# Attention on one core: the cast, the subtraction and the store of a chunk's output stand four head steps later

## The chip, the cores and the metric

The kernel runs on one core of one Trainium2 chip. The metric is the device time of one launch, in microseconds. Its engines are named as the profile names them: PE is TensorE's matmuls and PEld its weight loads, DVE is VectorE, ACT is ScalarE, POOL is GpSimd, and SP is SyncE, which here only issues DMAs. Each engine works through its own instructions in order and waits on semaphores.

## The reference

One post-norm decoder layer over `x` of shape (2, 2048, 512), 16 heads of 32. Only the first third matters here, causal self-attention:

```python
qkv = x @ Wqkv.T
q, k, v = map(merge_heads, jnp.split(qkv, 3, axis=-1))
dots = jnp.einsum('bhid,bhjd->bhij', q, k) * dh ** (-0.5)
dots = jnp.where(causal_mask, -jnp.inf, dots)
attn = jax.nn.softmax(dots, axis=-1)
out = jnp.einsum('bhij,bhjd->bhid', attn, v)
x = _layernorm(x + out @ Wout.T + bout)
```

A cross-attention over 77 context rows and a layer of 8 experts with top-2 gates follow, each with a residual and a norm.

## The kernel before

The program has three stages, one after the other. `project` makes queries, keys and values and leaves them in DRAM. `self_attention` makes the attention output and leaves it in DRAM as `o_parts`, in two float16 halves that together hold more than one float16 can. `second_half` does all the rest. The change lies in `self_attention`.

The work is cut into 8 groups: 2 sequences by 4 sets of 4 heads. A group's 2048 query columns are 4 chunks of 512 columns. Because the mask is causal, chunk `c` needs only the key tiles 0 to 4c+3 of 128 rows, so the chunks have 4, 8, 12 and 16 tiles, 40 in all. Each tile is done for 4 heads, which gives 160 head steps for a group. `KU` lists the tiles, `VU` the head steps. The chunks' last head steps are 15, 47, 95 and 159.

All engines walk through the same head steps `s`, each in its own function `step`. An item with lag L of head step p stands at `s = p + L`. The order is written out by hand with such lags:

- TensorE, lag 0 (`scores`, L865): keys times queries of one head and tile into one of three banks `st_ps`. It waits until the exponential three steps before has read its bank. Diagonal tiles get a mask by a second matmul (L868).
- ScalarE, lag 0 (L762): the exponential of that bank into `probs`. The buffer `probs` holds 5 tiles, and an exponential waits for the addition and the values product of the tile five before.
- GpSimd (L637): every fourth step it adds a tile of exponentials of all four heads onto `total`. Of the tiles off the diagonal each third is left to TensorE (L899), and a chunk's first tile is no addition of its own; the second tile's addition reads both.
- TensorE, `values` (L885) at lag 4 into `o_ps`, and `totals` (L909) at lag 12, which sums `total` over the rows for the softmax's denominators. `totals` waits for the last addition of the chunk.
- Besides, TensorE makes scores the other way round for later chunks (`aux`, L851) and VectorE takes row maxima of them (L804, L808), about one for each head step. A chunk's maxima are turned, cut in two by ScalarE and VectorE (L745, L797), and SP moves them into `q_pair` (`turn`, L678). They must be there before the chunk's first scores.

The end of a chunk is a chain over several engines, in lags after the chunk's last head step:

- `TAKEN` 5 and 13: ScalarE copies `o_ps` to `o_raw` (L768) and the denominators to `den` (L772).
- `DEN_MOVED` 14: SP moves the denominators to `inv_small` (L698). `INVERTED` 22: VectorE takes the reciprocals (L822). `INV_STORED` 24 and `INV_LOADED` 30: SP stores them to DRAM and loads them spread over the rows as `inv` (L702, L707).
- `SCALED` 38: GpSimd multiplies `o_raw` by `inv` into `o_sb` (L647), after the subtraction of the chunk before.
- `UPPER` 46: ScalarE casts `o_sb` to float16, the upper half of `o_out` (L777). It waits for the multiply.
- `LOWER` 49: GpSimd subtracts that upper half from `o_sb` into the lower half of `o_out` (L652). It waits for the cast.
- `STORED` 51: SP stores `o_out` to `o_parts` (L714). It waits for the subtraction.

`TAIL` is `STORED + 1`. The first `TAIL` steps run as a prologue, in which the maxima are spread evenly, and then come four laps of two groups each, all written out. SP also loads the next groups' keys and queries, one chunk at a time, at the absolute lags `REFILLED`: for a group's frame these stand at steps 54, 86, 93 and 100, the last with the values of the group (L666, L670). In the last lap at `s == TAIL` SP waits for the earlier laps' stores and issues `load_rows` (L941, L942), 2 MB for the next stage. `if REFILLED[c] <= TAIL: load(1, 1, c)` ahead of the laps covers a reload whose step falls into the prologue.

Of the kernel before, what the change touches and what calls it, by code (L numbers as in the profile page):

```python
# [401 lines left out]
def self_attention(nc, S, x_rows, q_parts, k_parts, v_rows, o_parts, inv_rows):  # L402
# [37 lines left out]
    INV_STORED = INVERTED + 2  # L440
    INV_LOADED = INV_STORED + 6
    SCALED = INV_LOADED + 8
    UPPER = SCALED + 8
    LOWER = UPPER + 3
    STORED = LOWER + 2
    TAIL = STORED + 1
# [81 lines left out]
    def chunk_at(s, lag, first, end):  # L528

        k = tile_at(s, lag, first, end)  # L530
        return k // NKU * CPB + CHUNK_OF[k % NKU] if k is not None and k % NKU in CHUNK_OF else None
# [11 lines left out]
    with ExitStack() as stack:  # L543
# [188 lines left out]
        def _(act):  # L732
# [15 lines left out]
            def step(i, s, first, end):  # L748
# [21 lines left out]
                if c is not None:  # L770
                    act.wait_ge(den_ready.sem, den_ready.at(i, c))
                    nc.scalar.activation(den[:, c % 2], den_ps[:], ACT.Copy, scale=1.0 / XS).then_inc(den_taken.sem, 1)  # L772
                c = chunk_at(s, UPPER, first, end)
                if c is not None:
# [744 lines left out]
def layer(nc, x_rows, xT, ctxT, mask, wqkvT, woutT, bout, wq, bq, wk, bk, wv, bv, wo, bo, w1, b1, w2, b2, centroids,  # L1519
          routeT, out):  # L1520

    dram = lambda name, shape, dt: nc.dram_tensor(name, shape, dt).ap()
    q_parts, k_parts, o_parts = (dram(n, [2, D, N], F16) for n in ("q_parts", "k_parts", "o_parts"))
    v_rows = dram("v_rows", [N, D], F32)
    inv_rows = dram("inv_rows", [2, HG, CH], F32)
    w_parts = dram("w_parts", [2 * KT, P, 2, KT * D], F16)
    k_blocks, v_ctx = dram("k_blocks", [B, P, NG * HG * S2], F32), dram("v_ctx", [B, S2, D], F32)
    with ExitStack() as stack:
        S = lasting(nc, stack)
        smalls = [(S["bout_bc"][:], bout.partition_broadcast(P)), (S["bo_bc"][:], bo.partition_broadcast(P)),  # L1530
                  (S["bq_sb"][:], bq), (S["b1_sb"][:], b1), (S["b2_sb"][:], b2)]
        project(nc, S, xT, wqkvT, ctxT, wk, wv, woutT, wq, wo, w1, w2, centroids, routeT, smalls, bk, bv,
                q_parts, k_parts, v_rows, w_parts, k_blocks, v_ctx)
        self_attention(nc, S, x_rows, q_parts, k_parts, v_rows, o_parts, inv_rows)
        second_half(nc, S, x_rows, o_parts, mask, w_parts, k_blocks, v_ctx, out)
# [68 lines left out]
```

## Time and profile before

| | |
|---|---|
| median of 3 runs | 2617.73 us (2617.07 to 2618.23) |
| the profiled execution's own time | 2619.38 us |
| its span | 2617.6 us |
| TensorE matmuls busy | 2421.4 us, 93% |
| VectorE busy | 1718.9 us, 66% |
| GpSimd busy | 1118.5 us, 43%, nearly all of it in the attention |
| ScalarE busy | 1102.5 us, 42% |
| attention | from about 285 to 1353 us of the span |

Busy shares are averages over the whole span, and the stages differ much, so the attention has to be read by itself. A line of a timeline begins with the start in microseconds from the start of the span and the duration. `x2` means two instructions merged into one line, and the brackets at the end give the idle time of the engine before it and what released it. Matmuls overlap in their ends, so a full PE row is not a full engine. The granted clock is a share of full speed: 1.00 is 2.4 GHz, 0.50 is 1.2 GHz.

### The profile page before, as it was taken

To read this page: it belongs to the slowest core of one execution; us is meant where nothing else is said; L and a number is where in the kernel's file an instruction comes from. 1 tells how busy PE (TensorE), PEld (TensorE's weight loads), DVE (VectorE), ACT (ScalarE), POOL (GpSimd) and SP (SyncE) were. 2 spreads that over 40 slices of the span, in tenths; PEclk is the share of its full clock that TensorE was granted. 3 is DMA by queue.
4 is the path that set the end of the run, shared out by engine and by line. 5 is a ranking of instruction groups with operands and counts; after the bars stand their busy time and mean duration, and the time that the engine had idled before them with its cause. 6 is when DMAs were issued, how large, how long until landed. Compare 5 with 4: busy or idle time off the path is not lost. (4 is left out here: it accounts for less than half of the span.)

```text
span 2617.6 us, 36273 instructions
## 1 busy us (share of the span) xinstructions
PE 2421.4 (93%) x13556; PEld 1013.8 (39%) x13556; DVE 1718.9 (66%) x3957; ACT 1102.5 (42%) x2066; POOL 1118.5 (43%) x404
## 2 busy tenths in 40 slices
PE   7999799999999999989946799999999999999998
PEld 3444223333323232323214354454445444454543
DVE  5433687777767677767405577767677776767665
ACT  4331156666666666666623242332324232322320
POOL 0000379989898989898952111102111211101100
PEclk9999799999999999999977899999999999999999
DMA  7864312212121213040021101010100101010000
GB/s 254 298 206 156 92 38 54 58 42 58 42 63 37 71 33 86 14 118 16 24 104 50 45 1 62 1 46 17 40 22 1 62 1 46 17 46 17 1 17 17
DMA packets 130443, 155.00 MB, mean 59 GB/s; under 512 B 19838, under 2 KB 98174, under 8 KB 129245
## 3 DMA queue, kind: packets, MB, share of 16 engines
q1 hardware_dynamic: 130269, 152.69, 19.1%
q8 instruction: 108, 1.77, 0.3%
q14 instruction: 66, 0.54, 0.1%
HBM read 99.96 MB, written 52.17 MB: 58 GB/s over the span
## 5 line engine op out<-in xcount | busy, mean ns | idle before, releaser
L762 ACT ACTIVATE probs<-st_ps 128x512 f32<-128x512 f32 (+3 forms) x1280 | 610.2, 535 | 339.9 <-PE st_ps L865 194.4
L637 POOL TENSOR_TENSOR total<-total,probs 128x2048 f32<-128x2048 f32 (+3 forms) x200 | 706.2, 3531 | 77.2 <-ACT probs L762 58.6
L804 DVE TENSOR_REDUCE seg_max<-s_ps 128x1 f32<-128x512 f32 x768 | 505.9, 685 | 139.2 <-PE s_ps L851 137.0
L865 PE MATMUL st_ps<-q_pair,k_pair 98*128 98x512 f16 (+3 forms) x1280 | 445.2, 362 | 34.9 <-ACT probs L762 28.8
L851 PE MATMUL s_ps<-k_pair,q_pair 96*128 96x512 f16 (+3 forms) x1280 | 446.1, 364 | 33.1 <-DVE seg_max L804 11.6
L1429 PE MATMUL fps<-x2T,w_p_hi 128*128 128x512 f16 x1024 | 317.3, 379 | 0.0
L885 PE MATMUL o_ps<-probs,v_sb 128*32 128x512 f32 (+3 forms) x2560 | 307.2, 553 | 0.0
L808 DVE CUSTOM_DVE_ANT_0 s_ps<-s_ps,later 128x384 f32<-128x384 f32 (+3 forms) x512 | 250.7, 497 | 85.8 <-issue 82.4
L1429 PE MATMUL fps<-w_p_hi,hT 128*128 128x512 f16 x1024 | 305.9, 380 | 0.0
L865 PEld LDWEIGHTS st_ps<-q_pair,k_pair 98*128 98x128 f16 x1280 | 125.0, 99 | 345.3 <-ACT probs L762 244.8
L1133 POOL TENSOR_TENSOR rstd<-rstd,keep_power 128x4 f32<-128x4 f32 x24 | 26.0, 1085 | 542.0 <-DVE rstd L1254 542.0
L1216 ACT ACTIVATE hidden<-fps,keep_b_sb 128x512 f32<-128x512 f32 x128 | 86.4, 686 | 377.0 <-PE fps L1429 374.8
L1148 POOL TENSOR_TENSOR soft<-soft,ssum 128x1232 f32<-128x1232 f32 x32 | 72.9, 2287 | 392.6 <-DVE ssum L1284 392.6
L851 PEld LDWEIGHTS s_ps<-k_pair,q_pair 96*128 96x128 f16 x1280 | 126.6, 100 | 235.6 <-DVE seg_max L804 119.5
L1391 DVE SCALAR_TENSOR_TENSOR x<-fps,gates_un,x 128x512 f32<-128x512 f32 x256 | 183.5, 742 | 34.4 <-PE fps L1429 31.5
L1429 PE MATMUL fps<-w_p_lo,hT 128*128 128x512 f16 x512 | 194.7, 380 | 0.0
L1429 PE MATMUL fps<-x2T,w_p_lo 128*128 128x512 f16 x512 | 194.0, 379 | 0.0
L1380 DVE TENSOR_SCALAR hT<-hidden 128x512 f16<-128x512 f32 x128 | 92.1, 719 | 105.7 <-ACT hidden L1216 105.0
L637 POOL TENSOR_TENSOR total<-probs 128x2048 f32<-128x2048 f32 (+1 forms) x32 | 136.4, 4263 | 46.4 <-ACT probs L762 46.4
L1429 PEld LDWEIGHTS fps<-x2T,w_p_hi 128*128 128x128 f16 x1024 | 100.1, 98 | 128.9 <-issue 5.9
L1429 PEld LDWEIGHTS fps<-w_p_hi,hT 128*128 128x128 f16 x1024 | 98.1, 98 | 131.0 <-issue 20.9
L1187 ACT ACTIVATE soft<-soft 128x1232 f32<-128x1232 f32 x32 | 39.4, 1231 | 201.0 <-DVE soft L1277 201.0
(164 smaller groups left out, 3403.5 us busy)
## 6 DMA issues: line engine op xcount, KB each, us to landing
k_pair<-k_parts SPq DMA_DIRECT2D x96, 128.0 KB, 3.9
q_pair<-q_parts SPq DMA_DIRECT2D x96, 128.0 KB, 4.9
x_raw<-xT_in SPq DMA_DIRECT2D x8, 1024.0 KB, 6.1
q_parts<-qk_out SPq DMA_DIRECT2D x32, 256.0 KB, 3.7
k_parts<-qk_out SPq DMA_DIRECT2D x32, 256.0 KB, 3.8
piece_raw<-w_in SPq DMA_DIRECT2D x8, 1024.0 KB, 8.7
v_rows<-v_out SPq DMA_DIRECT2D x32, 256.0 KB, 2.1
w_parts<-piece_cut SPq DMA_DIRECT2D x8, 1024.0 KB, 5.6
```

Source lines behind the costliest of these rows:

```text
L637: last = nc.gpsimd.tensor_tensor(summed[:, :, off:], other[:, :, off:], probs[:, k % NP, :, off:], ALU.add)
L762: nc.scalar.activation(probs[:, k % NP, h, off:], st_ps[:, p % (2 * NVU) % RING, off:], ACT.Exp, scale=SCALE).then_inc(exp_done.sem, 1)
L804: nc.vector.reduce_max(highest, s_ps[:, slot], AX.X).then_inc(s_read.sem, 1)
L808: nc.vector.tensor_tensor_reduce(s_ps[:, slot, 0:width], s_ps[:, slot, 0:width], later[:, CH - width:CH], 1.0, MASKED, ALU.add, ALU.max, h ...
L851: nc.tensor.matmul(s_ps[:, slot, 0:width], q_pair[a][0:NR, c, h, j * P:(j + 1) * P], k_pair[a][0:NR, h, s * CH:s * CH + width], start=True ...
L865: last = nc.tensor.matmul(st_ps[:, slot, off:], k_pair[a][:, h, kt * P:(kt + 1) * P], q_pair[a][:, c, h, off:], start=True, stop=not diagonal)
L885: last = nc.tensor.matmul(o_ps[out, off:], v_sb[a][:, kt, out], probs[:, k % NP, h, off:], start=(kt == 0), stop=final)
L1148: nc.gpsimd.tensor_tensor(soft[:, j], soft[:, j], ssum[:, j, :].rearrange("p (h a) -> p h a", a=1).broadcast_to([P, H, S2]), ALU.mult).the ...
L1216: nc.scalar.activation(hidden[:, n % 2], fps[:, (u * NUNIT + f) % FB], ACT.Gelu, bias=W["b1_sb"][:, n:n + 1], scale=UN).then_inc(gelu_done ...
L1380: nc.vector.tensor_scalar(hT[:, 0, e % 2, j], hidden[:, n % 2], XS, None, ALU.mult).then_inc(h_hi.sem, 1)
L1391: nc.vector.scalar_tensor_tensor(x2[q][:, j], bank, gates_un[q][:, j, e:e + 1], x2[q][:, j], ALU.mult, ALU.add).then_inc(added.sem, 1)
L1429: last = nc.tensor.matmul(bank, lhs(a, t), rhs(b, t), start=(n == 0), stop=(n == len(steps) - 1))
```

## The change

ScalarE's cast of a chunk's output stands at lag 50 instead of 46. `LOWER`, `STORED` and `TAIL` are set from it, so the subtraction moves from 49 to 53, the store from 51 to 55, and `TAIL` from 52 to 56. `SCALED` and everything ahead of it in the chain stay, and so do the reloads' lags. `REFILLED[0]` is 55, so `REFILLED[0] <= TAIL` now holds, and the reload of chunk 0 for the second group is issued ahead of the laps. Of items that share a step SP takes the reloads before the store.

```diff
     INV_STORED = INVERTED + 2
     INV_LOADED = INV_STORED + 6
     SCALED = INV_LOADED + 8
-    UPPER = SCALED + 8
+    UPPER = SCALED + 12
     LOWER = UPPER + 3
     STORED = LOWER + 2
     TAIL = STORED + 1
```

## Rows read from the trace of the kernel before

**Rows 1.** One window: us, busy us of PE, PEld, DVE, ACT, POOL, granted clock, DMA

```profile
400.00:1200.00 800.00, 763.38 (x4986) 243.81 (x4988) 587.97 (x1902) 511.88 (x1103) 724.20 (x239) 0.96 0.22 55
```

**Rows 2.** List of waits, 300 to 1400 us: total us, times, longest us

```profile
ACT o_out L777 <- POOL o_sb L647: 45.1, 17, 9.8
...
PE st_ps L865 <- ACT probs L762: 28.8, 17, 4.4
...
POOL total L637 <- ACT probs L762: 105.0, 49, 16.3
```

**Rows 3.** Timeline of ScalarE: start us, duration, operation, idle time before

```profile
515.91 0.45 ACT L762 ACTIVATE probs<-st_ps 128x128 f32<-128x128 f32 x2 [0.68 <-PE st_ps L868]
520.70 0.63 ACT L777 ACTIVATE o_out<-o_sb 128x512 f16<-128x512 f32 x1 [4.34 <-POOL o_sb L647]
...
523.68 0.60 ACT L762 ACTIVATE probs<-st_ps 128x512 f32<-128x512 f32 x1
```

**Rows 4.** Timeline of GpSimd, second group

```profile
519.41 1.26 POOL L647 TENSOR_TENSOR o_sb<-o_raw,inv 128x512 f32<-128x512 f32 x1
520.63 7.33 POOL L637 TENSOR_TENSOR total<-total,probs 128x1536 f32<-128x1536 f32 x3
...
529.02 4.52 POOL L637 TENSOR_TENSOR total<-probs 128x2048 f32<-128x2048 f32 x1
...
537.64 9.22 POOL L637 TENSOR_TENSOR total<-total,probs 128x2048 f32<-128x2048 f32 x2 [4.09 <-ACT probs L762]
...
590.75 4.53 POOL L637 TENSOR_TENSOR total<-probs 128x2048 f32<-128x2048 f32 x1 [2.05 <-ACT probs L762]
597.30 4.54 POOL L637 TENSOR_TENSOR total<-total,probs 128x2048 f32<-128x2048 f32 x1 [2.02 <-ACT probs L762]
```

**Rows 5.** Timeline of TensorE's matmuls, first, second and last group

```profile
396.29 0.39 PE L865 MATMUL st_ps<-q_pair,k_pair 98*128 98x512 f16 x1 [2.50 <-ACT probs L762]
...
521.55 0.61 PE L865 MATMUL st_ps<-q_pair,k_pair 98*128 98x512 f16 x1 [3.80 <-ACT probs L762]
...
528.33 1.94 PE L885 MATMUL o_ps<-probs,v_sb 128*32 128x512 f32 x8
...
533.61 1.04 PE L909 MATMUL den_ps<-total,ones 128*32 128x512 f32 x8
...
1338.20 1.94 PE L909 MATMUL den_ps<-total,ones 128*32 128x512 f32 x8 [11.54 <-POOL total L637]
```

**Rows 6.** Windows of 2 us in the second group (columns as in rows 1)

```profile
522.00:524.00 2.00, 2.00 (x10) 0.64 (x12) 1.24 (x6) 1.66 (x4) 2.00 (x1) 0.50 0.00 0
...
530.00:532.00 2.00, 1.78 (x9) 0.53 (x5) 0.73 (x3) 1.00 (x2) 2.00 (x1) 0.70 0.77 239
```

**Rows 7.** Timeline of VectorE: a masked maximum, 512 wide

```profile
525.88 0.69 DVE L808 CUSTOM_DVE_ANT_0 s_ps<-s_ps,later 128x512 f32<-128x512 f32 x1 [0.23 <-issue]
526.50 0.14 DVE L808 DVE_READ_ACCUMULATOR2_ANT seg_max<- 128x1 f32 x1
```

**Rows 8.** Two idle times of TensorE and the 3 us behind each

```profile
1179.35 0.34 PE L851 MATMUL s_ps<-k_pair,q_pair 96*128 96x384 f16 x1 [2.28 <-DVE seg_max L804]
...
1615.63 0.60 PE L1498 MATMUL cps<-keep_ident,gates 128*8 128x128 f32 x4 [1.60 <-DVE gates L1366]
...
1179.35:1182.35 3.00, 2.79 (x10) 0.83 (x14) 2.88 (x11) 1.19 (x2) 0.00 (x0) 0.57 0.10 29
1615.63:1618.63 3.00, 3.00 (x16) 1.52 (x17) 2.88 (x8) 1.87 (x2) 0.00 (x0) 1.00 0.02 5
```

**Rows 9.** SP's issue of the maxima's rows; their landing times (64 DMAs)

```profile
514.32 1.21 SPq L678 DMA_DIRECT2D q_pair<-max_rows  x2
...
DMA to landing us min/median/max: 1.7/1.9/9.1
```

**Rows 10.** Seventh group: SP's issue of load_rows and VectorE's wait

```profile
1124.84 0.39 SPq L941 DMA_DIRECT2D keep_x<-x_rows_in  x1
...
1137.11 0.25 DVE L822 RECIPROCAL inv_small<-inv_small 128x16 f32<-128x16 f32 x1 [4.86 <-DMA inv_small<-den]
```

## The prediction

> **What bounds the kernel now.** I read the window of the attention first. Over 800 us in its middle the matmul row is busy 763 us, GpSimd 724, VectorE 588 and ScalarE 512 [rows 1]. TensorE and GpSimd are both nearly full, so the question is which wait makes one stand while the other has work. The list of waits for 300 to 1400 us answers it: ScalarE stood 45.1 us in front of the very cast that is moved, 17 times, waiting for GpSimd's multiply `o_sb`; the matmuls stood 28.8 us behind ScalarE's exponentials, the largest wait of a matmul in the attention proper; and GpSimd itself waited 105.0 us for exponentials [rows 2]. So GpSimd is late at some places and idle at others.
>
> The timeline of one group (a group is 160 head steps, 126.7 us; this is the second of eight) shows the loop. A chunk's last step is 15, 47, 95 or 159 of its group. With `UPPER` = 46 the cast of chunk 1 stands at step 93, GpSimd's multiply for it (`SCALED` = 38) at step 85. ScalarE ended the exponential of step 93 at 516.36 us and then stood 4.34 us for the multiply, which began at 519.41 and ended at 520.67 [rows 3, 4]. TensorE may be only three score banks ahead (`RING` = 3), so it ran dry: 3.80 us idle [rows 5]. After it the granted clock was 0.50 of full (1.2 GHz, not 2.4) until about 531 us [rows 6]; eight values matmuls took 1.94 us there [rows 5]. Groups 2 to 5 repeat this; the first has a smaller wait, 2.50 us [rows 5], and a shorter slow stretch.
>
> Chunks 0 and 2 find their multiply done. For chunk 3 of the group before, ScalarE hardly stands. The longest of the 17 waits, 9.8 us [rows 2], is at the end, after all scores, where nothing is left to delay but the chain itself.
>
> **The change, part by part.** `UPPER` goes from 46 to 50, `LOWER` 49 to 53, `STORED` 51 to 55, `TAIL` 52 to 56. No instruction is added or removed in the steady part: 32 casts, 32 subtractions, 32 stores as before.
>
> *ScalarE.* The cast of chunk 1 stands at step 97, behind four more exponentials: 94 and 95, 128 wide, whose scores were there (0.56 us together), and 96 and 97, 512 wide at 0.60 us [rows 3], the first a microsecond after 516.4 because its scores come behind a values step. ScalarE is at the cast at about 518.7 instead of 516.4, and the multiply still ends at 520.67: a wait of 2.0 us is left of 4.34. TensorE meanwhile can issue scores up to step 100 instead of 96. In this stretch VectorE paces it too: one 512-wide masked maximum takes 0.69 + 0.14 us [rows 7]. I put TensorE's idle time at 1.7 us. Then, does the clock fall? Idle 2.28 us was followed by 0.57 of full clock, idle 1.60 us by 1.00 [rows 8], the same seven times over in the second half. 1.7 is by far nearer to the second, so I take: it stays high.
>
> By the Trainium skill (TensorE: Matmul & The Clock Gate, "What's actually happening") throttled is the default state and activity releases it, which speaks against counting on a rest of idle time being free. The rows agree that long idle times end at the lower level; they also show that short ones don't. If the page's warning held for this rest, rival B below would be the result.
>
> *What limits the gain.* GpSimd. From 597.30 us it runs without a gap through chunk 1's multiply to the last addition of chunk 2; in the group shown this chain ends 520.63 + 7.33 = 527.96 us. TensorE needs that sum at step 107 (`TOTALS`) and was there at 533.61 [rows 4, 5]. It can come 5.65 us earlier and no more. Does it? After the cast (521.3 us) ScalarE owes the exponentials 98 to 104 and one copy at 0.55 to 0.60 us; scores 104 come at about 524.6 instead of 530.2 (528.33 + 1.94), the totals at about 527.4. That is just under GpSimd's 527.96. So GpSimd decides, TensorE stands some 0.5 us more, and the gain is 5.65 us. Of it 3.8 us is the stall and 1.85 us the slow clock.
>
> Is it given back? GpSimd waits for exponentials three times later in the group: 4.09, 2.05 and 2.02 us [rows 4], beside two short waits. It loses these waits as ScalarE comes earlier, so it is 4.0 us earlier at 537.64 and 5.6 by 597.30, where it meets ScalarE again, with 2.5 us or more of idle time left. Exponentials wait for additions five tiles back; for tile 29 that addition ends at 529.02 + 4.52 = 533.54, and its exponential would come at about 535.6. Both sides hold. The gain repeats in each group.
>
> *GpSimd's queue.* The subtraction (1.16 us) moves four steps. For chunks 1 and 3 the step passed (100, 52) begins a chunk and has no addition, so its place is the same. For chunks 0 and 2 it comes after one addition of 4.5 us. All sums needed later come the same or 1.2 us earlier. Chunk 3's subtraction stands directly before chunk 0's multiply, which waits for it; its cast comes about 3 us before it is wanted. Nothing.
>
> *SP's queue.* SP runs ahead of the others and stands only on its waits, so an order change moves DMAs a lot. Chunk 3's store (step 54) now stands behind the reload of chunk 0 (also 54), and chunk 1's store (102) behind the reload of chunk 3 and the values (100). These reloads go out about 11 us earlier, and the rows behind the values' 1 MB no longer wait. Chunk 0's store (70) is released 4.5 us later, and behind it stand chunk 1's `inv_rows` store and load, used 15 us later, and the reload of chunk 1: 768 KB that now leave just ahead of the maxima's rows at 514.32 us. Those rows took 1.9 us to land in the median and 9.1 at worst [rows 9]. A lateness of up to 2 us vanishes in ScalarE's remaining wait. I take nothing for it.
>
> *Seventh group.* There `load_rows` (2 MB) stood at step 52 in front of the 768 KB reload, both in front of chunk 1's denominators; VectorE stood 4.86 us for them and TensorE 3.95, and a further 2.28 later [rows 8, 10]. Now the reload leaves before. 768 KB less in front is about 3.4 us (2.8 MB took 12.3 us from 1124.84 to 1137.1). With GpSimd's gaps there (2.5 and 3.8 us) I take 7 us for the group, between 4 and 8.
>
> *First and last group.* First: 2.5 us. The first 56 steps now carry 101 maxima tiles instead of 96 over 52; VectorE paces them either way, and the second chunk's rows come a step later: a loss of 0 to 1 us, I take 0.5. One 768 KB reload moves to the start, when the other loads are done. Last: TensorE ends waiting 11.54 us for GpSimd's total [rows 5], which has had no gap since the 2.0 us one early in that group. ScalarE's wait in it is worth 0: GpSimd is the bound to the end.
>
> *Sum.* 2.5 + 5 x 5.3 (5.65 less 0.35 for the handover from GpSimd) + 7 + 0 - 0.5 = 35.5; I round it down to 34.5 for places where the three engines nearly tie. The profiled execution took 2619.4 us for a span of 2617.6: 2584.9 by its own time, 2583.2 from the median of the runs, 2617.7. I say 2585.
>
> **Rivals.**
> A, the above: 2577 to 2592. Chance 0.57.
>
> B, *the clock still falls* at the remaining wait. For it: the level fell after 2.28 us and my 1.7 is an estimate. Then the 1.85 us of slow clock stay in six groups, and the time past step 107 loses perhaps as much again in half of them: 34.5 less 11 to 17, so 2595 to 2602. Chance 0.18.
>
> C, *the wait only moves*: exponentials run faster than I think between 516 and 519, or earlier gains eat the four steps, so that about 3 us of ScalarE wait stay. The gain is 1.5 to 2.5 us in a group: 2600 to 2608. Against it: four exponentials take at least 0.56 + 2 x 0.60 = 1.76 us [rows 3]. Chance 0.11.
>
> D, *GpSimd is the bound throughout*, and its work is the same: within 2 us of 2617.7. Against it: 8.2 us of waits in the group shown [rows 4]. For it: some of them may be forced by the order. Chance 0.06. The Trainium skill (Perfetto Trace Analysis, "Identifying the Most-Contended Engine") takes occupancy as a fair measure for GpSimd and not for matmuls, and would name GpSimd here; it would give this rival's time if taken for every stretch. The trace has GpSimd at 91% and waiting, so it agrees in part only.
>
> E, *slower*: the maxima's rows of chunk 3 land late because the reload of chunk 1 now goes just before them. At 9.1 us, 7.2 over the median, 2.0 are absorbed; 5.2 us of idle time and 1.85 of slow clock stand against 5.65 saved, so 1.4 us lost in each of seven groups: 2628. It decides from about 7.7 us to landing. Chance 0.04. The remaining 0.04 is for gains by ways that I don't see.
>
> **Numbers.** Range 2576 to 2603: A, B and the nearer part of C, 0.8. Differences under 0.2% (5 us) can't be told from no change. Faster 0.90 (A, B, C and the rest), same 0.06 (D), slower 0.04 (E).
>
> **What the changed kernel's profile would show.** ScalarE's wait before the cast falls from 45.1 to 20 to 28 us, 9.8 of them at the end; TensorE's wait for exponentials from 28.8 to under 15; the slices' clock near 1.0 through the attention; GpSimd's waits for exponentials from 105 to about 65; a new wait of 0 to 1 us before the totals of chunk 2; the step from one group's totals to the next 121 us instead of 126.7. I am wrong if the clock still drops once a group, if TensorE waits long for `max_rows`, or if GpSimd's gaps stay as they are.

## The result, and the profile after

| | before | changed |
|---|---|---|
| median of 4 runs each | 2617.98 us (2617.07 to 2622.35) | 2584.26 us (2582.06 to 2586.10) |
| span of the profiled execution | 2617.6 us | 2582.4 us |
| ratio | | 0.987, 95% interval 0.9856 to 0.9885 |

The forecast was 2585, the range 2576 to 2603. The changed kernel is faster, by 33.7 us in the medians.

The list of waits of the changed kernel for 300 to 1400 us (us in total, times, longest) answers to [rows 2]:

```profile
ACT o_out L777 <- POOL o_sb L647: 23.0, 9, 9.9
PE st_ps L865 <- ACT probs L762: 16.5, 16, 3.0
PE den_ps L909 <- POOL total L637: 13.3, 6, 10.9
ACT probs L762 <- POOL total L637: 6.3, 4, 3.0
PE st_ps L865 <- issue: 5.0, 1, 5.0
POOL total L637 <- ACT probs L762: 68.0, 25, 18.2
```

ScalarE stood 23.0 us before the cast instead of 45.1, TensorE 16.5 behind exponentials instead of 28.8, GpSimd 68.0 instead of 105.0. The third line is new in its length: TensorE now stands for GpSimd's sum at the totals, 10.9 us of it at the very end.

The timeline of the changed kernel shows the same place of the second group as [rows 3, 5], then two of GpSimd's waits that answer to [rows 4]:

```profile
518.88 0.63 ACT L777 ACTIVATE o_out<-o_sb 128x512 f16<-128x512 f32 x1 [1.55 <-POOL o_sb L647]
...
520.05 0.39 PE L865 MATMUL st_ps<-q_pair,k_pair 98*128 98x512 f16 x1 [1.34 <-ACT probs L762]
...
526.21 1.07 PE L909 MATMUL den_ps<-total,ones 128*32 128x512 f32 x8 [0.49 <-POOL total L637]
...
583.38 4.53 POOL L637 TENSOR_TENSOR total<-probs 128x2048 f32<-128x2048 f32 x1 [1.49 <-ACT probs L762]
589.94 9.21 POOL L637 TENSOR_TENSOR total<-total,probs 128x2048 f32<-128x2048 f32 x2 [2.03 <-ACT probs L762]
```

And its windows there, with the columns of [rows 1], then the long window that answers to [rows 1]:

```profile
520.00:522.00 2.00, 1.95 (x10) 0.50 (x14) 1.30 (x7) 2.00 (x5) 2.00 (x1) 1.00 0.56 144
522.00:524.00 2.00, 1.71 (x14) 0.42 (x7) 1.73 (x9) 1.94 (x4) 1.86 (x2) 1.00 0.87 178
...
400.00:1200.00 800.00, 777.43 (x5239) 251.33 (x5242) 610.09 (x1975) 535.06 (x1158) 755.14 (x251) 1.00 0.22 55
```

In this group the cast waits 1.55 us, TensorE 1.34 instead of 3.80, and the clock stays at full (2.4 GHz) where it was at half. The totals come 7.40 us earlier in the trace (533.61 less 526.21), and GpSimd's busy time in the 800 us rises from 724 to 755.

The clock did not stay up in every group. The mean of 800 us rounds to 1.00 and hides two short falls to half, in groups 3 and 6, behind idle times of TensorE of 1.52 and 1.69 us. The first of them in the timeline, then windows of the two groups:

```profile
641.49 0.39 PE L865 MATMUL st_ps<-q_pair,k_pair 98*128 98x512 f16 x1 [1.52 <-ACT probs L762]
...
642.00:644.00 2.00, 2.00 (x13) 0.40 (x12) 1.86 (x8) 2.00 (x5) 1.86 (x2) 0.71 0.89 174
644.00:646.00 2.00, 2.00 (x12) 0.49 (x5) 0.37 (x3) 0.76 (x2) 2.00 (x1) 0.50 0.87 132
...
1008.00:1010.00 2.00, 2.00 (x10) 0.31 (x10) 1.37 (x6) 1.36 (x3) 1.86 (x2) 0.52 0.69 122
```

In groups 2, 4, 5 and 7, behind 1.34, 1.58, 1.19 and 1.63 us, it stayed at full.

To see where the time came from, I take the starts of the matmuls of L909 and subtract them from the same ones of the kernel before. One number for each group, at the totals of its chunk 2 (10 steps after the place that the cast of chunk 1 has now) and of chunk 3:

| us earlier than before | group 1 | 2 | 3 | 4 | 5 | 6 | 7 | 8 |
|---|---|---|---|---|---|---|---|---|
| changed, chunk 2 | 0.79 | 7.40 | 11.93 | 17.03 | 22.02 | 26.34 | 30.40 | 35.59 |
| changed, chunk 3 | 1.88 | 7.37 | 11.93 | 17.01 | 21.99 | 26.34 | 34.43 | 34.39 |

So the groups gave 1.9, 5.5, 4.6, 5.1, 5.0, 4.4, 8.1 and nothing; of groups 2 to 6 the two that gave least, 3 and 6, are those in which the clock fell. Apart from the first, the seventh and the last group, the lead grows only between the totals of a group's chunk 3 and those of the next one's chunk 2, the stretch in which the cast stands, and is kept for the rest. The first totals of all are 2.68 us later than before, so the first group made some 4.5 us and lost 2.7.

### The profile page after: what moved, and what is told of

Same layout as the page of the kernel before. It is cut to its first block and busy times, and to the rows that moved or that the text cites. A ratio compares the mean times of both kernels' runs of the same rounds, so it can differ in the third digit from the quotient of the medians.

```text
span 2582.4 us, 36273 instructions
## 1 busy us (share of the span) xinstructions
PE 2400.6 (93%) x13556; PEld 1007.0 (39%) x13556; DVE 1714.1 (66%) x3957; ACT 1102.6 (43%) x2066; POOL 1118.8 (43%) x404
## 5 line engine op out<-in xcount | busy, mean ns | idle before, releaser
L851 PE MATMUL s_ps<-k_pair,q_pair 96*128 96x512 f16 (+3 forms) x1280 | 435.0, 355 | 25.9 <-DMA q_pair<-q_parts 11.4
L865 PE MATMUL st_ps<-q_pair,k_pair 98*128 98x512 f16 (+3 forms) x1280 | 434.4, 353 | 25.7 <-ACT probs L762 16.5
```

The costliest lines, as they stand in the source:

```text
L851: nc.tensor.matmul(s_ps[:, slot, 0:width], q_pair[a][0:NR, c, h, j * P:(j + 1) * P], k_pair[a][0:NR, h, s * CH:s * CH + width], start=True ...
L865: last = nc.tensor.matmul(st_ps[:, slot, off:], k_pair[a][:, h, kt * P:(kt + 1) * P], q_pair[a][:, c, h, off:], start=True, stop=not diagonal)
```

## The experiments

The theory with which I went in: the cast's place makes the whole gain, because it takes away TensorE's idle time and the slow clock, and GpSimd's chain sets its size. The rivals: that the subtraction, the store and `TAIL` do part of it, and that the remaining wait, not GpSimd, sets the size. The theory fell with the first run.

**The cast alone**

```diff
-    UPPER = SCALED + 8
-    LOWER = UPPER + 3
-    STORED = LOWER + 2
+    UPPER = SCALED + 12
+    LOWER = SCALED + 11
+    STORED = SCALED + 13
```

> ScalarE's cast alone stands four steps later; GpSimd's subtraction, the store and TAIL stay. Theory 1 (the cast's place in ScalarE's queue is the cause): groups 0 to 5 gain as in the changed kernel, some 27 us, the start loses nothing, and the seventh group keeps VectorE's 4.9 us wait for the denominators and gains 0 to 2 us. About 2590 us; ScalarE's wait before the cast 20 to 25 us. Theory 2 (SP's order, with reloads 11 us earlier, is the cause): no change in the middle groups, 2616 to 2620 us.

Measured: 2616.39 us against 2620.28 for the kernel before beside it, ratio 0.9985 (0.9976 to 0.9995). Most of the gain isn't there: 2590 was expected by the first theory. The time is the one that the second theory gave, but not its picture of middle groups without a change. ScalarE's wait before the cast is down to 21.5 us. From its list of waits:

```profile
DVE inv_small L822 <- DMA inv_small<-den: 94.6, 10, 47.5
PE s_ps L851 <- DVE seg_max L804: 26.0, 36, 3.8
POOL total L637 <- ACT probs L762: 99.7, 53, 15.8
```

In the changed kernel the first of these is 66.4 us, 3 times. The numbers at L909 say where it goes: at chunk 2 this kernel is ahead by 2.84, 6.23, 6.46, 5.83 and 5.38 us in groups 2 to 6, but at the chunk 3 right behind only by 0.93, 1.36, 0.79, 1.05 and 2.23. It makes 4 to 6 us in each group and gives 2 to 6 back before the next totals. The timeline of SP, VectorE and TensorE of this kernel in the fourth group, where most is given back:

```profile
781.44 0.38 SPq L714 DMA_DIRECT2D o_parts<-o_out  x1
781.86 1.44 SPq L666 DMA_DIRECT2D k_pair<-k_parts  x3
783.34 1.38 SPq L666 DMA_DIRECT2D q_pair<-q_parts  x3
784.76 0.43 SPq L670 DMA_DIRECT2D v_sb<-v_rows  x1
785.24 5.92 SPq L678 DMA_DIRECT2D q_pair<-max_rows  x2
791.20 0.59 SPq L698 DMA_DIRECT2D inv_small<-den  x1
...
795.34 0.25 DVE L822 RECIPROCAL inv_small<-inv_small 128x16 f32<-128x16 f32 x1 [4.63 <-DMA inv_small<-den]
...
796.20 0.34 PE L851 MATMUL s_ps<-k_pair,q_pair 96*128 96x384 f16 x1 [3.80 <-DVE seg_max L804]
```

And its window behind the last line, with the columns of [rows 1]:

```profile
798.00:800.00 2.00, 2.00 (x11) 0.24 (x9) 1.55 (x5) 1.01 (x2) 0.77 (x1) 0.50 0.24 88
```

SP takes its items in order. Its store of chunk 1 waits for GpSimd's subtraction, which ends at 781.4. Behind it stand the reload of chunk 3, the values, two moves of maxima and the denominators of chunk 2. The two moves of maxima take 5.92 us to issue instead of the 1.16 of the changed kernel, and their maxima were ready at 779.7 us, so this is no wait for them; what differs is that the reload and the values' 1 MB were issued just in front. So the denominators leave at 791.20 and VectorE stands 4.63 us for them. Until then it frees no bank of the scores made the other way round, and TensorE stands 3.80 us for VectorE. The stall that the cast's place took away is back 22 us after its old place, at a granted clock of 0.50. In groups 1 to 6 VectorE's wait is 1.82 to 4.63 us.

The kernel before has the same order in SP's queue. Its fourth group:

```profile
786.86 5.53 SPq L678 DMA_DIRECT2D q_pair<-max_rows  x2
792.43 0.59 SPq L698 DMA_DIRECT2D inv_small<-den  x1
...
797.01 0.25 DVE L822 RECIPROCAL inv_small<-inv_small 128x16 f32<-128x16 f32 x1
```

The denominators left 1.23 us later there, but VectorE came to the reciprocals only at 797.01 us and did not wait for them. In the first and the seventh group it did wait, 1.42 and 3.11 us:

```profile
417.31 0.25 DVE L822 RECIPROCAL inv_small<-inv_small 128x16 f32<-128x16 f32 x1 [1.42 <-DMA inv_small<-den]
1178.50 0.25 DVE L822 RECIPROCAL inv_small<-inv_small 128x16 f32<-128x16 f32 x1 [3.11 <-DMA inv_small<-den]
```

These are the groups with the short stall at the cast (2.50 us) and with none of a microsecond or more.

**The subtraction, the store and `TAIL` without the cast** (`UPPER = SCALED + 8`, `LOWER = SCALED + 15`, `STORED = SCALED + 17`)

> The cast stays at its place; the subtraction, the store and TAIL stand four steps later. Theory 1: the 3.8 us idle time and the slow clock stay once a group, ScalarE's wait stays near 45 us; only the seventh group gains, 6 to 8 us, and the start loses 1 to 2. About 2612 us. Theory 2 (SP's order is the cause): near 2584 us.

Measured: 2615.22 us, ratio 0.9984 (0.9974 to 0.9993). ScalarE's wait before the cast is 48.3 us, TensorE's for exponentials 27.3. Through groups 2 to 6 it stays within 1 us of the kernel before; in the profile its 4 us come in the seventh group, where 6 to 8 were expected. So one part alone gives 4 us, the other alone 5, and both together 34.

**Cast and reload, all else as before.** The edit of the cast alone, and the reload of chunk 3 with the values four steps earlier, which puts it ahead of chunk 1's store:

```diff
-    REFILLED = [DEN_MOVED + n for n in (41, 73, 80, 87)]
+    REFILLED = [DEN_MOVED + n for n in (41, 73, 80, 83)]
```

> The kernel before with the cast alone four steps later and the reload of chunk 3 with the values at head step 96 in place of 100, so ahead of chunk 1's store (step 98) in SP's queue. Cast alone gained 5 to 5.7 us at every group's totals of chunk 2 and lost it again within 12 steps, where VectorE waits for the denominators that stand in the queue behind 1.8 MB of reload. Theory A (that queue is the whole of the loss): the gain stays in all groups, the second stall of the seventh group goes too; the first, at step 69, stays: 2586 to 2594 us. Rival B (something else in the later store or subtraction is needed): near cast alone, 2610 to 2617.

Measured: 2584.89 us, ratio 0.987 (0.9855 to 0.9885), the whole gain, a microsecond more than the expectation. SP in its fourth group:

```profile
771.37 0.38 SPq L714 DMA_DIRECT2D o_parts<-o_out  x1
771.79 1.16 SPq L678 DMA_DIRECT2D q_pair<-max_rows  x2
772.99 0.59 SPq L698 DMA_DIRECT2D inv_small<-den  x1
```

Now the moves take 1.16 us, and the denominators leave 1.6 us behind the store instead of 9.8.

**Cast and values only.** The cast alone, and the values loaded with chunk 2 instead of chunk 3 (`if c == CPB - 2:`); the keys and queries of chunk 3 stay behind the store.

> Cast alone four steps later, and the 1 MB of values loaded with the reload of chunk 2 (step 93) in place of chunk 3's (100), so ahead of the store; the 768 KB of chunk 3 stay behind it. If the values' 2048 short pieces hold the queue (the maxima's rows take 5.6 us to issue behind them), most of the gain stays: 2588 to 2600 us. If 768 KB are enough to make the denominators late: 2605 to 2617.

Measured: 2585.12 us, ratio 0.9868 (0.9853 to 0.9883). SP in the fourth group:

```profile
772.08 1.38 SPq L666 DMA_DIRECT2D q_pair<-q_parts  x3
773.50 1.15 SPq L678 DMA_DIRECT2D q_pair<-max_rows  x2
774.69 0.59 SPq L698 DMA_DIRECT2D inv_small<-den  x1
```

The moves take 1.15 us although 768 KB still stand just in front of them. So the 768 KB alone don't hold them up, and the values' 1 MB has to be there too. Whether the values would do it alone no run shows.

**The changed kernel with that reload behind the store again**

```diff
-    REFILLED = [DEN_MOVED + n for n in (41, 73, 80, 87)]
+    REFILLED = [DEN_MOVED + n for n in (41, 73, 80, 91)]
```

> The changed kernel with only the reload of chunk 3 and the values put back behind chunk 1's store (step 104 in place of 100). Theory A: VectorE waits 2 to 4.5 us for the denominators once a group again, and about 5 us a group are given back: 2606 to 2616 us, the seventh group's first stall stays away. Rival B: 2584.

Measured: 2613.17 us, ratio 0.9977 (0.9968 to 0.9986). 6 us of the gain are left. SP and TensorE in the timeline of its fourth group:

```profile
784.37 0.43 SPq L670 DMA_DIRECT2D v_sb<-v_rows  x1
784.85 5.81 SPq L678 DMA_DIRECT2D q_pair<-max_rows  x2
790.70 0.59 SPq L698 DMA_DIRECT2D inv_small<-den  x1
...
795.67 0.34 PE L851 MATMUL s_ps<-k_pair,q_pair 96*128 96x384 f16 x1 [3.66 <-DVE seg_max L804]
```

And from its list of waits:

```profile
DVE inv_small L822 <- DMA inv_small<-den: 90.5, 10, 47.6
```

The same stall at the same place. The four runs agree from both sides: the gain is there when the values leave ahead of chunk 1's store, and gone when they leave behind it.

**Cast and store moved, the subtraction not** (`UPPER = SCALED + 12`, `LOWER = SCALED + 11`, `STORED = SCALED + 17`)

> Cast and store (with TAIL) four steps later, the subtraction at its old place. Both theories of SP's order: as the changed kernel, 2583 to 2586 us. Rival (the subtraction's place matters for GpSimd's queue): 5 us or more slower than that.

Measured: 2587.03 us, ratio 0.9877 (0.9861 to 0.9894). That is 2.8 us above the changed kernel and 1 above what was expected, with intervals of the ratios that overlap. In the profiles the last totals are 1.65 us behind those of the changed kernel. The clock fell in other groups here (2, 4 and 7), so the profile doesn't settle whether the subtraction's place has a part in it.

**The cast two steps later still** (`UPPER = SCALED + 14`, `LOWER` and `STORED` as in the changed kernel)

> The cast at lag 52 in place of 50; subtraction, store and TAIL as in the changed kernel. Theory 1 (GpSimd's sum of chunk 2 decides, the 1.3 to 1.7 us that TensorE still idles at the cast are not lost twice): the wait at the cast falls to below 0.7 us a group and TensorE waits 1.5 to 2 us more at the totals instead; time within 3 us of the changed kernel, 2581 to 2587. Rival (the remaining wait at the cast costs what it shows): 1.3 us less in each of seven groups, about 2575. Rival (the idle time, now in one piece before the totals, drops the clock): 2590 to 2596.

Measured: 2582.93 us, ratio 0.9859 (0.9842 to 0.9875), no different from the changed kernel. ScalarE's wait before the cast goes from 23.0 to 12.9 us and TensorE's for exponentials from 16.5 to 7.5, but TensorE's wait for GpSimd at the totals grows from 13.3 to 18.6. The wait that is left at the cast costs nothing that these times show; GpSimd's chain is the bound.

**All of it by two steps instead of four** (`UPPER = SCALED + 10`, the rest behind it as before)

> The cast at lag 48, half the way (subtraction 51, store 53, TAIL 54). ScalarE gains only the two 128-wide exponentials, 0.5 us, so it waits about 3.8 us; TensorE can issue two more steps, about 1 us, and idles about 2.8 us. Theory 1 with the clock as a term: the clock still falls once a group, each middle group gains about 1 us and the seventh its 6 to 8: 2603 to 2608 us. Rival (the gain goes with the steps): half of it, about 2600, with the clock up in most groups.

Measured: 2600.3 us, ratio 0.9926 (0.9911 to 0.994), 20 us or some six tenths of the gain. My theory said 2603 to 2608, the rival 2600 with the clock up in most groups; the time is the rival's, and the clock fell in every one of groups 2 to 6. The stall of the second group in its timeline, and the window behind it:

```profile
518.98 0.39 PE L865 MATMUL st_ps<-q_pair,k_pair 98*128 98x512 f16 x1 [3.34 <-ACT probs L762]
...
520.34 0.63 PE L865 MATMUL st_ps<-q_pair,k_pair 98*128 98x512 f16 x1
```

```profile
520.00:522.00 2.00, 2.00 (x9) 0.73 (x6) 1.37 (x7) 1.37 (x4) 1.86 (x2) 0.50 0.72 135
522.00:524.00 2.00, 2.00 (x13) 0.57 (x11) 1.83 (x10) 1.79 (x4) 1.86 (x2) 0.77 0.88 191
```

TensorE is idle for 3.34 us, and a microsecond after it starts again the granted clock is 0.50. Two steps shorten this stall by 0.5 us and the slow stretch behind it by more: it is over before 524 us here, and was 0.70 between 530 and 532 us in the kernel before [rows 6]. The theory had only counted whether the clock falls, not for how long.

**GpSimd relieved of one tile.** The changed kernel, with tile 7 of chunk 2 left to TensorE's L899:

```diff
-    POOLED = [[n for n, (k, kt) in enumerate(KU) if k == c and (kt >= c * TT or kt % 3 != 2)]
+    POOLED = [[n for n, (k, kt) in enumerate(KU) if k == c and (kt >= c * TT or (kt % 3 != 2 and (c, kt) != (2, 7)))]
```

> The changed kernel, with one tile of chunk 2 (the eighth) summed by TensorE in place of GpSimd: 4.5 us less for GpSimd, 0.9 us more for TensorE in each group. Theory (GpSimd's chain decides when TensorE may pass the totals of chunk 2): the waits at the cast of chunk 1 go away, the period of a group falls by 1 us, and the last group, bound by GpSimd to the end, by 3 to 5 us: 2572 to 2578. Rival (TensorE is the bound by now): 0.9 us more in each group, about 2590.

Measured: 2573.93 us, ratio 0.9829 (0.9814 to 0.9843), 10 us better than the changed kernel. ScalarE waits before the cast only at the end (9.7 us, once), TensorE 3.4 us for exponentials, and a group takes about 120 us. GpSimd's waits are back at 100.6. GpSimd has 4.5 us of work less in a group, TensorE a little more, and TensorE is now the bound. So GpSimd was the bound of the changed kernel where the clock stayed up. A part of the 10 us is the clock, which doesn't fall in groups 2 to 7 of this kernel.

In its first group it loses ground at one place, a late move of maxima and a slow clock behind it, here in the timeline and in a window:

```profile
397.59 0.39 PE L865 MATMUL st_ps<-q_pair,k_pair 98*128 98x512 f16 x1 [1.59 <-DMA q_pair<-max_rows]
...
402.00:404.00 2.00, 2.00 (x9) 0.57 (x11) 1.70 (x10) 1.61 (x3) 0.30 (x1) 0.50 0.78 191
```

The changed kernel has no such wait there and a full clock. Against it this kernel is 0.7 us ahead at the totals of chunk 1 and 4.1 behind at those of chunk 2.

**The reload of chunk 0 in its step instead of ahead of the laps**

```diff
+                    if first is not None and s == REFILLED[c] - 1:
+                        load(1, 1, c)
```

and without the lines ahead of the laps.

> The changed kernel, with the first reload of chunk 0 back at head step 54 of the first group in place of ahead of the laps. Theory: this reload, issued right behind the first rows of maxima, made them land late; TensorE's idle time before the first scores falls from 5.0 to 3.4 us and all later comes 1.6 us earlier: about 2582.6 us. Rival (the loss at the start is from the other spread of the maxima, or from outside the attention): no difference, 2584, and 5.0 us stays.

Measured: 2582.44 us, ratio 0.986 (0.9843 to 0.9876); span 2578.5 against 2582.4. The medians are 1.8 us apart, with intervals that overlap. The first scores in its timeline:

```profile
303.80 0.58 PE L866 MATMUL st_ps<-q_pair,k_pair 98*128 98x512 f16 x1 [3.50 <-issue]
```

The changed kernel's:

```profile
305.96 0.58 PE L865 MATMUL st_ps<-q_pair,k_pair 98*128 98x512 f16 x1 [5.00 <-issue]
```

Six kernels with the reload ahead of the laps stood 4.4 to 5.0 us here, eight without it 2.9 to 3.7. So 768 KB more at the start cost 1 to 2 us.

**Both of these**

> The changed kernel with both edits, the reload in its step and one tile of chunk 2 to TensorE. If both theories hold, their gains add up: 2570 to 2577 us.

Measured: 2572.87 us, ratio 0.9823 (0.9808 to 0.9838), the fastest of the study: 11.4 us under the changed kernel and 45 under the one before.

**`load_rows` four steps later in the kernel before** (`if end is not None and s == TAIL + 4:`)

> The kernel before, with load_rows four steps later (head step 56 in place of 52 of the last lap), so that the reload of chunk 0 goes out ahead of it; nothing else is moved. Theory (the seventh group's 8 us come from SP's order): the store of the group before still stands in front of both, so VectorE's wait for chunk 1's denominators falls only in part: 1 to 8 us less, 2610 to 2617. Rival (they come from the cast): no difference, 2618.

Measured: 2618.09 us, ratio 0.9999 (0.9989 to 1.0008). The expected 1 to 8 us did not come. The profile shows VectorE's wait for the denominators in the seventh group at 3.90 us instead of 4.86. The store of the chunk before, with its wait, still stands in front, so the reload, `load_rows` and the denominators still leave one behind the other within 5 us.

## Why the prediction was right, and where it wasn't

*The time and its terms.* 2585 was said, 2584.26 came. Summed for the groups: 2.5 less 0.5 at the start was said and 1.9 came; 5 x 5.3 = 26.5, and 24.5 came (5.5, 4.6, 5.1, 5.0, 4.4); 7, and 8.1 came; 0, and 0. That makes 34.4 us against the 34.5 used and the 35.5 of the sum. The rounding down "for places where the three engines nearly tie" was in the right direction, but what it met in groups 3 and 6 was the clock. That the sum fits so well is luck in part: two of its steps, on the clock and on SP's queue, don't hold as written, as told below.

*ScalarE.* A wait of 2.0 us was forecast to be left, and 1.55 was; in groups 2 to 7 it was 1.40 to 1.90 us. TensorE's idle time was put at 1.7 and was 1.34 (1.19 to 1.69 in groups 2 to 7). Its wait for exponentials in all was said to fall under 15 us and was 16.5. The stall stood in groups 2 to 6 before, not 2 to 5; the sum has five groups all the same.

*The clock: right in four groups of six.* The prediction took the 1.7 us to be like an idle time of 1.60 us in another stage, and so "it stays high". It did in groups 2, 4, 5 and 7. In groups 3 and 6 it fell to half 1.3 and 1.6 us after the matmuls had started again, behind 1.52 and 1.69 us. The group's step, from one group's first totals to the next, says what that cost: 121.4 us where the clock stayed up, 122.1 and 122.0 in these two, so 0.6 to 0.7 us each and not the 1.85 that the prediction had taken from the kernel before. 121 was said. So rival B, which priced a fall in all six groups, is wrong in its time, but what it warned of is there. The line of the Trainium skill that the prediction weighed (TensorE: Matmul & The Clock Gate, "What's actually happening", activity releases the throttle) agrees with the two-step kernel, which was at 0.50 behind 3.34 us of idle time, and with groups 3 and 6 here. In the last group a wait of 3.00 us was left, with the clock at 0.60 behind it, and cost nothing, since GpSimd was the bound there.

*GpSimd as the limit.* The "new wait of 0 to 1 us before the totals of chunk 2" was 0.49 us, with the totals 7.40 us ahead, 5.5 of it made in this group. It came in all of groups 1 to 7 but 3 and 6, where the slow clock made TensorE the later one. Moving the cast further brought 1.3 us between medians whose intervals overlap, and relieving GpSimd 10. Rivals C and D are out. Its waits fell to 68.0 where about 65 was forecast.

*"Both sides hold" for tile 29.* They didn't quite. The changed kernel's timeline shows the exponential waiting for the addition in three of the groups, as here in the first:

```profile
419.67 1.09 ACT L762 ACTIVATE probs<-st_ps 128x512 f32<-128x512 f32 x2 [1.10 <-POOL total L637]
```

I had 2.1 us of margin on paper and 1.1 us of lateness in those groups. The totals show no loss from it.

*The subtraction* was taken at nothing. Left in its place it gave 2587.03; that nothing became up to 3 us can't be excluded.

*SP's queue: the step that failed.* The prediction had seen the right fact: the reloads "go out about 11 us earlier, and the rows behind the values' 1 MB no longer wait". Then it said "I take nothing for it", and put the gain down to the cast. The runs show that this is a condition of the gain and not an extra. In the kernel before, TensorE and VectorE came some 5 us late to the reciprocals of chunk 2 because of the stall at the cast, and the late denominators were hidden behind it. Once the stall goes, they are next: with the cast alone only 4 us are left of 34, and with the reload put back behind the store 6. The sum came out right because the four steps moved the store too, which the prediction had not counted on: that is luck. The trace of before would have shown it. VectorE's wait of 3.11 us for these denominators, in the seventh group, stands right in front of the 2.28 us of TensorE's idle time that the prediction took for its clock [rows 8]. I asked what a longer wait in SP's queue would cost and did not ask which transfer would be late once TensorE came 5 us earlier.

*Seventh group.* 7 us said, 8.1 measured, for the reason given: the denominators' wait there went from 4.86 to 0.68 us. In the kernel with cast and reload moved but `load_rows` in its old place it stayed, at 4.59. The rows of the changed kernel:

```profile
1098.48 0.40 SPq L941 DMA_DIRECT2D keep_x<-x_rows_in  x1
1099.48 0.57 SPq L698 DMA_DIRECT2D inv_small<-den  x1
...
1106.57 0.25 DVE L822 RECIPROCAL inv_small<-inv_small 128x16 f32<-128x16 f32 x1 [0.68 <-DMA inv_small<-den]
```

*The start.* 0.5 us of loss was said, from 0 to 1. The first totals came 2.68 us late. Some 1.6 are TensorE's longer wait before the first scores, 5.00 us where the kernel before had 3.37; this is the reload that the prediction placed "when the other loads are done". Another 1.55 lie ahead of the attention, whose first matmul started at 287.32 instead of 285.77 us; other kernels of the study show such a shift without the reload, so it isn't the change's. The first group made this up with some 4.5 us.

*Rival E.* TensorE's waits for `max_rows` were 0.9 us at most. Excluded here.

*What stays open.* Why the clock fell behind some idle times of 1.5 to 1.9 us and not behind others; whether the values alone hold up the moves behind them; why the maxima come late in the first group of the kernel with the tile moved; and whether the subtraction's place is worth a microsecond or two.

## What to carry to other kernels

Two stalls in series can hide each other: take away the first, and the second gives the gain back 22 us later. The trace of before shows it only where the first is short or missing, here in two groups of eight, so read the odd groups too and not only the one that repeats. And for each queue ask not only what the moved instruction delays, but what in it would be late if the bound engine came earlier by the whole gain; here that was a small transfer behind an in-order store and 1 MB of loads. When a moved step takes others with it, try the move of each one alone: 4, 5 and 34 us say more than the total. A mean that rounds to 1.00 over a long window is no proof of a clock that never fell: look at the stretch behind each stall.

## What the runs showed of the hardware

The issue of a DMA on SP is not of fixed length. Two moves of maxima took 1.16 us to issue when the values' 1 MB had been issued 8 us before, 1.15 with 768 KB of keys and queries just in front, and 5.81 and 5.92 us with those 768 KB and the values' 1 MB just in front; over the groups of the three kernels with that order whose lines stand above, 3.20 to 6.32. What is behind them in SP's queue is late by that too.

TensorE's granted clock was at half or near it behind idle times of 3.00, 3.34 and 3.80 us. Behind shorter ones it went both ways. In the changed kernel 1.19, 1.34, 1.58 and 1.63 us left it at full and 1.52 and 1.69 did not; in the kernel with cast and reload moved, the 4 us behind 1.88 us of idle time at 519.79 had 0.64, those behind 1.89 us at 764.11 had 1.00. So the length of the last idle time alone does not decide it here. The fall can come after work has resumed: in one case of 3.34 us the first matmuls behind still took 0.39 us, as at full speed, and those a microsecond later 0.63.
